# The attention's output product of a macaron block in three rounded passes instead of one fp32 product

## The reference

```
x = x + 0.5 * ffn(layernorm(x))
x = x + attn(layernorm(x))
x = x + 0.5 * ffn(layernorm(x))
attn(y) = y + (softmax(causal(q k^T / 8)) v) @ Wo,   q, k, v = y @ Wq, y @ Wk, y @ Wv
```

## Time and profile before

| | before |
|---|---|
| median of 3 runs | 1531.22 us |
| the profiled execution | 1531.53 us |
| its span | 1529.7 us |
| PE busy | 1457.3 us (95%) |
| DVE busy | 1072.6 us (70%) |
| ACT busy | 813.9 us (53%) |
| POOL busy | 293.5 us (19%) |
| fp32 product with wo, L516 | 128 records, about 592 ns each |

### The profile page before, as it was taken

One profiled execution on the slowest core, in us unless ns is written; L12 is line 12 of the kernel. 1 busy time (PEld: TensorE's weight loads), 2 busy tenths in 40 slices (PEclk: granted clock), 3 DMA queues, 4 the chain that ended last, 5 costly groups with the idle time before them and its releaser, 6 DMA issues.

```text
span 1529.7 us, 29784 instructions
## 1 busy us (share of the span) xinstructions
PE 1457.3 (95%) x9664; PEld 973.4 (64%) x9664; DVE 1072.6 (70%) x2413; ACT 813.9 (53%) x1912; POOL 293.5 (19%) x589
## 2 busy tenths in 40 slices
PE   2999999999989999999999999999889999999998
PEld 1666666666655666665666666666556666666665
DVE  6977877788666666666666575666568777777775
ACT  3444333433457777777777677777743344333422
POOL 2100000000114434334344344344310000000000
PEclk9999999999999999999999999999999999999999
DMA  5443333333300000000000000000023333333333
GB/s 180 130 164 110 106 103 113 105 112 95 113 21 1 1 2 2 2 1 3 2 2 1 3 1 3 1 1 1 1 72 107 111 126 103 118 105 123 106 122 85
DMA packets 58867, 97.94 MB, mean 64 GB/s; under 512 B 6144, under 2 KB 15360, under 8 KB 58752
## 3 DMA queue, kind: packets, MB, share of 16 engines
q1 hardware_dynamic: 58752, 96.44, 19.9%
HBM read 92.75 MB, written 3.67 MB: 63 GB/s over the span
## 4 chain that ended last, share of the span: by engine, by line
PE 49%; issue 30%; POOL 16%; DVE 4%; DMA 1%; ACT 0%; POOLq 0%; SPq 0%; DVEq 0%
PE banks L374 17%; POOL work L1291 16%; PE banks L196 9%; PE banks L198 9%; PE banks L197 9%; PE banks L336 1%; PE banks L346 1%; DVE work L1097 1%; DVE work L1069 1%; PE banks L503 0%; POOL pool_pace L1286 0%; DVE bn L907 0%; DMA bias<-in_gate_bias 0%; DMA work<-cw_rows 0%; POOL aw_lo L1280 0%
## 5 line engine op out<-in xcount | busy, mean ns | idle before, releaser
L725 ACT ACTIVATE work<-banks 128x512 f32<-128x512 f32 x336 | 200.5, 597 | 462.4 <-PE banks L198 444.2
L374 PE MATMUL banks<-work,wd 128*128 128x512 f32 x672 | 342.9, 593 | 0.3 <-DVE work L1097 0.3
L1069 DVE TENSOR_TENSOR work<-banks,work 128x512 f32<-128x512 f32 x336 | 231.9, 690 | 153.0 <-ACT work L725 148.1
L780 ACT ACTIVATE work<-banks,nmax 128x512 f32<-128x512 f32 (+3 forms) x512 | 263.7, 526 | 39.3 <-DVE nmax L1153 39.2
L1291 POOL TENSOR_SCALAR work<-work,rrec 128x512 f32<-128x512 f32 (+3 forms) x512 | 261.6, 533 | 1.6
L196 PE MATMUL banks<-xT_hi,wg_hi 128*128 (+1 forms) x336 | 247.9, 738 | 0.0
L1097 DVE TENSOR_TENSOR work<-work 128x512 f32<-128x512 f32 x320 | 225.7, 705 | 15.8 <-DVE work L1069 9.3
L1168 DVE COPY stage<-banks 128x1024 f32<-128x1024 f32 (+1 forms) x128 | 122.0, 953 | 128.0 <-PE banks L489 128.0
L1153 DVE TENSOR_REDUCE nmax<-banks 128x2 f32<-128x1024 f32 (+3 forms) x256 | 196.0, 808 | 6.4 <-PE banks L478 6.3
L374 PEld LDWEIGHTS banks<-work,wd 128*128 128x128 f32 x672 | 126.3, 189 | 33.4 <-issue 2.2
L196 PE MATMUL banks<-xT_hi,wu_hi 128*128 (+1 forms) x336 | 133.3, 397 | 0.0
(11 more groups left out here) (122 smaller groups left out, 2215.0 us busy)
## 6 DMA issues: line engine op xcount, KB each, us to landing
work<-cw_rows SPq DMA_DIRECT2D x320, 256.0 KB, 3.1
x<-in_x SPq DMA_DIRECT2D x8, 256.0 KB, 7.0
out_rows<-x SPq DMA_DIRECT2D x8, 256.0 KB, 2.2
cw_rows<-cwT SPq DMA_DIRECT2D x16, 96.0 KB, 1.9
stage<-in_w_gate SPq DMA_DIRECT2D x3, 448.0 KB, 5.7
stage<-in_w_up SPq DMA_DIRECT2D x3, 448.0 KB, 6.4
wd<-in_w_down SPq DMA_DIRECT2D x3, 448.0 KB, 7.3
stage<-in_wq SPq DMA_DIRECT2D x1, 512.0 KB, 3.8
```

Of the source, the lines that this page charges most:

```text
L374: pe.matmul(psY, wd[:, j * P:(j + 1) * P], z[part_slot(j)], start=j == 0, stop=j == HT - 1, skip_group_check=True).then_inc(s["down_ps"], 1)
L725: nc.scalar.activation(silu[j % 2], psG[j % 3], ACT.Silu) \
L780: m = nc.scalar.activation(prob[:, p % 2, i, o:o + w], ps[:, i, so:so + w], ACT.Exp, bias=nmax[:, p % 2, i, qb:qb + 1], accum_out=rsum[:, ...
L1069: tt(gated[j % 3], psU[j % 3], silu[j % 2], ALU.mult) \
```

## The change

The product with Wo is made by `mm3`. ACT writes the weighted sum rounded (`ctx_parts[0]`, semaphore `ctx_hi`), DVE its remainder (`ctx_parts[1]`, `ctx_lo`) as the first instruction of its slot. PE's waits on `ctx_sb` become waits on `ctx_lo`. Wo is loaded as a fourth part of the staged attention weights and split with them: ACT in tile 14, POOL behind it; PE's first projection waits for `aw_lo` 4. The buffer `wo` goes. To make room, `small` shrinks to 224 columns (112 KB); the halves (768 columns, 384 KB) come in a transfer of their own into a work buffer, issued behind `bias`, with a semaphore of their own.

```diff
-SMALL = 7 * P + E + TB * G * G
+SMALL = P + E + TB * G * G
...
-        aw = [sb(f"aw_{n}", [P, 3, H * DK], F32R) for n in ("hi", "lo")]
-        wo = sb("wo", [P, H * DK])
+        aw = [sb(f"aw_{n}", [P, 4, H * DK], F32R) for n in ("hi", "lo")]
...
+        half_f32 = work[:, 5 * CH:5 * CH + 6 * P]
...
-        ctx_sum = sb("ctx_sum", [P, CH])
+        ctx_parts = [sb(f"ctx_{n}", [P, CH], F32R) for n in ("hi", "lo")]
...
-            sp.dma_start(small[:, :], small_in).then_inc(s["consts_loaded"], 16)
+            sp.dma_start(small[:, :], small_in[:, 0:SMALL]).then_inc(s["consts_loaded"], 16)
             load_x(sp, 0)
             sp.dma_start(gate_w[:, :], gate_in).then_inc(s["consts_loaded"], 16)
             sp.dma_start(bias[:, :], bias_in.partition_broadcast(P)).then_inc(s["consts_loaded"], 16)
+            sp.dma_start(half_f32, small_in[:, SMALL:]).then_inc(s["half_loaded"], 16)
             load_group(sp, 0)
...
-            sp.dma_start(wo[:, :].rearrange("p (j d) -> p j d", d=P),
+            sp.dma_start(attn_w[:, 3, :].rearrange("p (j d) -> p j d", d=P),
...
-                    pe.wait_ge(s["aw_lo"], 3)
+                    pe.wait_ge(s["aw_lo"], 4)
...
-                pe.wait_ge(s["ctx_sb"], n + 1)
+                pe.wait_ge(s["ctx_lo"], n + 1)
...
-                pe.matmul(psO, wo[:, p * P:(p + 1) * P], ctx_sum[:, :], start=p == 0, stop=p == HP - 1,
-                          skip_group_check=True).then_inc(s["out_ps"], 1)
+                c = slice(p * P, (p + 1) * P)
+                mm3(pe, psO, [w[:, 3, c] for w in aw], [t[:, :] for t in ctx_parts], p == 0, p == HP - 1) \
+                    .then_inc(s["out_ps"], 1)
...
-                    if std_n == 3 and j >= AW_SLOT and j - AW_SLOT < 3:
+                    if std_n == 3 and j >= AW_SLOT and j - AW_SLOT < 4:
...
-                nc.scalar.activation(ctx_sum[:, :], psA, ACT.Copy).then_inc(s["ctx_sb"], 1)
+                nc.scalar.activation(ctx_parts[0][:, :], psA, ACT.Copy).then_inc(s["ctx_hi"], 1)
...
+            def ctx_low(b, p):
+                n = pair(b, p)
+                dve.wait_ge(s["ctx_hi"], n + 1)
+                tt(ctx_parts[1][:, :], psA, f32(ctx_parts[0][:, :]), ALU.subtract).then_inc(s["ctx_lo"], 1)
+
...
                 have_q = not (last and p + 2 >= HP)
+                if not (first and p < 2):
+                    ctx_low(*ahead(b, p, -2))
                 if not (first and p < 1):
                     pT_copy(*ahead(b, p, -1), 1, first and p < 3)
...
                     attn_slot(NC - 1, p, False, True)
+                ctx_low(NC - 1, HP - 2)
                 pT_copy(NC - 1, HP - 1, 1, False)
                 for k in list(ROUTING)[6:]:
                     ROUTING[k](NC)
+                ctx_low(NC - 1, HP - 1)
                 add_out(NC - 1)
...
-            nc.vector.tensor_copy(half[:, :], small[:, P:7 * P])
+            dve.wait_ge(s["half_loaded"], 16)
+            nc.vector.tensor_copy(half[:, :], half_f32)
...
-            for w in range(3):
+            for w in range(4):
                 pool.wait_ge(s["aw_hi"], w + 1)
```

More of the change, by code:

```diff
@@ L64, in constants @@
     tie = np.broadcast_to((np.arange(G)[None, :] < np.arange(G)[:, None]), (P, TB, G, G))
-    small = np.concatenate([ident, *halves, iota, tie.reshape(P, -1)], 1)
+    small = np.concatenate([ident, iota, tie.reshape(P, -1), *halves], 1)
     return small.astype(np.float32)
@@ L90, in build @@
         ident = small[:, 0:P]
-        iota = small[:, 7 * P:7 * P + E]
-        tie = small[:, 7 * P + E:].rearrange("p (t a b) -> p t a b", t=TB, a=G)
+        iota = small[:, P:P + E]
+        tie = small[:, P + E:].rearrange("p (t a b) -> p t a b", t=TB, a=G)
         half = sb("half", [P, 6 * P], BF16)
@@ L100, in build @@
         stage_flat = stage[:, :, :, :].rearrange("p a b c -> p (a b c)")
-        attn_w = stage_flat[:, 0:3 * H * DK].rearrange("p (w c) -> p w c", w=3)
+        attn_w = stage_flat[:, 0:4 * H * DK].rearrange("p (w c) -> p w c", w=4)
         pT = stage_flat[:, 0:4 * PW].rearrange("p (r c) -> p r c", r=2)
-        aw = [sb(f"aw_{n}", [P, 3, H * DK], F32R) for n in ("hi", "lo")]
-        wo = sb("wo", [P, H * DK])
+        aw = [sb(f"aw_{n}", [P, 4, H * DK], F32R) for n in ("hi", "lo")]
         work = sb("work", [P, 14 * CH])
@@ L168, in build @@
         psT, psA, psO = pairs[2], bank[6], bank[7]
-        names = """consts_loaded attn_w_loaded
+        names = """consts_loaded half_loaded attn_w_loaded
             stat_dve stat_act stat_rows stat_bn
@@ L178, in build @@
             q_ps k_ps v_ps q_hi q_lo k_hi k_lo v_sb s_ps max_done exp_done rec_done norm_done
-            pT_ps pT_act pT_dve ctx_ps ctx_sb out_ps outT_sb outT_ps out_added stored""".split()
+            pT_ps pT_act pT_dve ctx_ps ctx_hi ctx_lo out_ps outT_sb outT_ps out_added stored""".split()
         s = {n: sem("s_" + n) for n in names}
@@ L572, in attn_slot @@
                 else:
-                    pe.wait_ge(s["ctx_sb"], n - 1)
+                    pe.wait_ge(s["ctx_lo"], n - 1)
                 if p == 4 and not last:
```

## The result

| | before | after |
|---|---|---|
| median (fastest to slowest, runs) | 1531.15 us (1530.01 to 1531.66, 4) | 1539.33 us (1538.24 to 1540.35, 4) |
| the profiled execution | 1531.53 us | 1538.24 us |
| its span | 1529.7 us | 1536.5 us |

The ratio is 1.0054, 95% interval 1.0037 to 1.0072: slower, and beyond the upper end of the predicted range (1538.5). The profiled executions are 6.7 us apart; the same kernel run again on another occasion gave a ratio of 1.0045 (1.0031 to 1.0058), 6.9 us by the ratio and 5.7 by the medians. So 6 to 7 us have to be explained, where the prediction had 2.6. The miss of the range is narrower than that of the sum: the medians are 8.2 us apart here, the profiles 6.7, and on the second occasion the changed kernel's median was 1537.56 us, inside the range.

A forecast was written before the change was run, and what follows sets the result against it. In ordinary attention slots the chain through ACT and DVE to k_lo, level with PE's work, was taken to end last. Terms -1.2 + 3.0 + 1.3 + 1.1 + 1.0 - 2.6 = +2.6 on 1531.2 gave 1533.8 us, range 1528.0 to 1538.5.

The forecast's parts named there:

- constants, start: At the program's start, the smaller first transfer lets the bias land and DVE begin earlier: -2.6 us.
- p = 4: Attention slot p = 4 of seven chunks, where the product is on the way: 0.17 us less each, -1.2 us.
- loop slots: Attention slots with evacuation late at ACT's loop: the remainder delays the copy, 0.75 us each, +2.25 for three.
- first pairs: Late evacuation at 469.03, first of four such slots: the remainder delays the copy PE needs, +0.75 us.
- last chunk and tail: Last attention chunk, where PE waits for DVE: remainders delay it, +1.3 us in the slots and +1.1 in the tail.
- fourth split: Feed-forward tile 14, last chunk: POOL's added subtraction holds DVE's product L1097 and delays the first projection, +1.0 us.
- rival B: The start gives only 0.9 us, since the bias still queues, now with the halves: 1535.5 us; chance 0.20.
- A: Rival: PE's saving in the output product counts in every attention slot, 1524.1 us; chance 0.12.
- C: Rival: the remainder does not fit in the ordinary attention slot; at 0.1 us over, 1539.2 us; chance 0.10.
- D: Rival: ACT's loop stalls fall elsewhere and cost nothing, 1531.5 us, no change; chance 0.08.

The follow-up runs named there:

- e5: The kernel before with only the smaller first transfer and the halves in a transfer of their own, product still fp32: 1530.68 us, ratio 0.9991.
- e4: The changed kernel with one rounded pass instead of three in the output product, remainder still made and waited for: 1542.52 us, ratio 1.0066.
- e10: The changed kernel with a fourth pass, remainder by remainder, in the product with Wo: 1538.37 us, ratio 1.0049.
- e9: The changed kernel run again, unchanged: 1537.56 us, ratio 1.0045 to the kernel before.
- e11: The kernel before run again, unchanged: 1531.69 us, ratio 0.9997 to its other runs.
- e3: The changed kernel without DVE's remainder of the weighted sum, PE's three passes reading the rounded part in its place: 1531.47 us, ratio 1.0003.
- e8: The kernel before, product in fp32, with gate_w and bias out of DVE's start wait and its three splits spread out: 1528.87 us, ratio 0.9973.
- e1: The changed kernel with the transfers of bias and gate_w issued in the other order: 1535.07 us (one run).
- e2: The changed kernel with the remainder behind the copy in slots where evacuation is late or PE waits for DVE: 1536.6 us, ratio 1.0033.
- e6: The changed kernel with the four weight splits in tiles 2, 5, 8 and 11 instead of 11 to 14: 1538.05 us, ratio 1.0038.
- e7: The changed kernel with splits spread, remainder behind the copy in late slots, gate_w and bias out of DVE's start wait: 1532.0 us, ratio 0.9991.

## Why the prediction was wrong

It missed the profiled difference by 4.1 us (+6.7 against +2.6), step by step, in us:

| step | predicted | measured | miss |
|---|---|---|---|
| constants, start | -2.6 | -0.9 | +1.7 |
| evacuation 2 to 58: p = 4 | -1.2 | -0.5 | +0.7 |
| evacuation 2 to 58: loop slots | +2.25 (three) | +3.0 (1.84 in the three, 1.19 in two more) | +0.8 |
| late evacuation, first pairs | +0.75 | +0.78 | 0.0 |
| last chunk and tail | +2.4 | +2.9 | +0.5 |
| fourth split | +1.0 | +1.26 | +0.3 |
| up to the first evacuation | 0 | +0.1 | +0.1 |

**The step that failed first is the landing of the bias**, put at -2.6 us and measured at -0.9: "with 384 KB fewer ahead of it the bias should do at least as well: 1.9. Since gate_w's 3.3 itself contains the wait behind small's 496 KB, I take 2.6". The trace of before had the warning, which rival B named: the bias took 1.9 us longer than gate_w with only 16 KB between them, so what made it late was not the big transfer in front. What the smaller first transfer gave is what gate_w gained, 1.0 us; the bias landed as long after gate_w as before (2.5 and 2.4 us). It landed at 6.5, the value from which B decides, and B's 0.9 us is what came (1.2 in e5 alone). The exact figure is luck, since this landing scatters by 1.75 us over the eight profiles; the failure is not, since none of them starts before 5.70 where 4.8 was forecast. I gave B 0.20 and my own term 0.50; the row spoke for B.

**p = 4** was mis-sized: the 0.17 us are real on PE, but I read idle time only at the next instruction, not up to the end of the slot, where k_lo is waited for. ACT's work does not move (k_hi starts 0.87 us after the product's start in both kernels, held by the copy of v in front of it), so k_lo doesn't either. e4 and e10 bound it from both sides in six of the slots: 0.46 us less of PE gives nothing more, 0.23 more costs 0.14. In the seventh, in the first chunk, all of it counts (-0.18, and by e4 and e10 -0.24 and +0.23).

**The loop slots**: in the three that I counted the copy moved by what the sum says, and the slots lost 0.54 to 0.66 us of the 0.75. (The first of the four in the prediction, evacuation 0 at 469.03, is late not by ACT's loop but because it stands behind a table load of 1.28 us, at 467.62, and the std; its 0.75 came whole.) But two more lost time, those of evacuation 22 and 38. There PE's loop comes round as well and PE is the late one. Timeline of the kernel before, ACT, PE and DVE, then of after:

```profile
697.67 0.60 ACT L802 ACTIVATE ctx_sum<-banks 128x512 f32<-128x512 f32 x1 [1.23 <-issue]
...
697.94 0.50 PE L468 MATMUL banks<-k_hi,q_hi 64*128 64x512 f32 x2 [1.57 <-issue]
...
699.65 0.69 DVE L1168 COPY stage<-banks 128x512 f32<-128x512 f32 x1 [3.84 <-PE banks L489]
```

```profile
699.57 0.50 PE L469 MATMUL banks<-k_hi,q_hi 64*128 64x512 f32 x2 [1.54 <-issue]
...
699.79 0.69 DVE L1175 TENSOR_TENSOR ctx_lo<-banks,ctx_hi 128x512 fp32r<-128x512 f32 x1 [2.32 <-ACT ctx_hi L804]
...
701.28 0.69 DVE L1170 COPY stage<-banks 128x512 f32<-128x512 f32 x1 [0.80 <-PE banks L490]
...
702.70 0.40 PE L490 MATMUL banks<-small,work 64*128 64x64 f32 x6 [0.38 <-issue]
```

The remainder is over 0.80 us before the copy's release here, so it isn't in the way; what is new is a second stop of PE, 0.38 us for no wait at all, in the middle of its transposes, and in the slot of evacuation 38 a longer first one (1.85 where it was 1.57). e9 has both again, 0.21 and 1.70. But these two slots vary without any remainder, and the profile of before that everything is measured from is the shortest of its kind. Against it, the slot of 22 is longer by 0.39 us in e11, 0.27 in e3, 0.29 in e5 and 0.31 in e8, and that of 38 by 0.06 in e3, 0.24 in e5 and 0.26 in e8; while e1, which has the remainder, lost only 0.12 in that of 38. On the mean of the kernels without the remainder (leaving out e11 for 38, which has a half-clock stretch there), 0.25 of the 0.60 us and 0.14 of the 0.59 are not the remainder's. The second stop of PE shows in five of the eight profiles with the remainder and in none of the five without; what brings it no run shows, and how these two slots lose the rest stays open. In the three counted slots there is no such doubt: the kernels without the remainder lie between 0.22 us shorter and no longer than before, those with it in DVE's first place 0.45 to 0.69 us longer.

**Last chunk and tail**: the terms came out nearly as summed but for one stretch at half clock. Slots 4 to 7 were to cost 1.3 and cost 1.22 (slot 4 alone 1.03, of which 0.60 is PE's wait; slot 7 did not wait longer), the last attend was to move by 0.5 and the last evacuation came 0.56 later. Behind that evacuation the prediction has 0.6 of its 1.1; it was 1.14 in the first profile and 0.56 in the second. The first has a stretch at half clock at 1135 us which the second lacks, and that is the whole miss of 0.5 (e1 and e2 have one there too and take 18.8 us from the last evacuation into the third stage; e6, e7 and e9 have none and take 18.2). How much of the 1.22 is the remainder's own isn't settled. The stretches at half clock come at the same places of the work in both profiles of the changed kernel (1084, 1111 and 1121 us; 1082, 1109 and 1120), but at others in the kernel before (1080 and 1114 to 1121); and e8, without a remainder, lost 2.3 us in this chunk, where e11 gained 0.95.

**The fourth split**: DVE made up 0.2 of the 1.47 us it lost, not 0.4. POOL was ready first, and the row decided. By the rule of the Trainium skill that was weighed there ("SBUF — State Buffer", section on the engine ports), whoever starts first holds the shared pair for a whole instruction. The trace agrees: the 2.05 and 2.16 us both end 0.55 us after POOL's subtraction beside them does (at 418.24 and 421.03). The rule's other case, DVE first, did not come.

**The rivals.** A (PE's saving counts everywhere, 1524.1) falls by e4: 0.46 us less per pair and no gain in the ordinary slots. C (the remainder doesn't fit an ordinary slot) falls by the 0.22 us to spare. D (the loop stalls fall elsewhere) falls: the slots of evacuation 14, 30 and 46 came late in every profile. B was right in its figure for the start; that the halves behind the bias hold it up, as B says, no run shows by itself. With B's start the profiled execution would be at 1535.8, still 2.4 under the 1538.2, by the other misses in the table.

**The range** was 1 us too short at the top. Each term's bounds were written down, and most of the misses lie inside them (start 0.9, loop slots up to 1.3 each, last chunk up to 3.5): all five fell on the slow side, and a range built as if they would cancel didn't hold that. That it was passed by only 0.8 us, and in e9 not at all, hangs on half-clock stretches as much as on the steps.

## What to carry to other kernels

A rounded three-pass product in place of an fp32 one trades PE time for an operation on the engine that makes the remainder. Where the chain through that engine is the one that ends last, the PE time is worth next to nothing (here not even when two of the three passes are gone) and the operation costs nearly in full wherever a slot starts late, so count first the slots in which its cover is short. A transfer that is needed late should not be in the wait that starts the program: taking two out of it was worth more than shrinking the one ahead of them. Of a saved instruction ask what the next wait of the same slot is, up to its last instruction, not only whether there is idle time behind it.

## What the runs showed of the hardware

- A 16 KB transfer that spreads one row over 128 partitions landed 4.3 us after issue in fourth place (3.5 to 5.2 over ten profiles) and 2.6 in third; a plain one of 16 KB 3.0 and 2.3. Its landing moved DVE's start between 5.70 and 7.45 us over eight profiles.
- The half-clock stretches (3.4 or 6.8 us long) come at other places in another execution of the same program: 17.1 and 13.7 us in two profiles of before, 20.5 and 13.7 in two of after. The one near 445 us is in all, as 3.4 or 6.8 us, and by itself makes the way to the first evacuation 34.3 or 35.1 to 35.6 us.
- The kernel with the least PE work was the slowest, with the most half clock (30.7 us) in its profile. Whether less work brings more such stretches isn't shown: one more pass (e10) had as much as none (e9).
- PE stops when its loop comes round (1.5 to 2.1 us that no wait explains, in stretches at full clock), and can stop a second time (0.2 to 0.5 us) some 3 us later. ACT's stop at its own loop took 1.0 to 1.4 us.
